# The end of a decoder layer: indirect gathers moved ahead and joined, the last two normalisation roots moved from GpSimd to ScalarE and VectorE, the last dense step split by tiles

## The chip, the core and the metric

The kernel runs on one core of a Trainium2 chip. The metric is the device time in microseconds of one execution, the median of several runs. Engines are called by the names of the profile: PE (TensorE), DVE (VectorE), ACT (ScalarE), POOL (GpSimd) and SP (SyncE, which issues plain DMAs here).

## What is computed

Input x has 8 sequences of 256 tokens with 128 features: 2048 tokens, which the kernel holds as 16 tiles of 128 tokens, in 4 groups of 4 tiles. Three layers follow one another, each with a residual and a layer norm: four blocks of elementwise linear attention with feed-forward, a cross attention with 16 heads, and a causal self attention with 16 heads and rotary positions, which is followed by a mixture of 31 experts of which each token takes its best 3, plus one shared expert. What the change touches is the end of that last layer:

```python
gates = jnp.sum(jax.nn.one_hot(topi, E_R, dtype=aff.dtype) * topv[..., None], axis=-2)
h = jax.nn.gelu(jnp.einsum('bsd,edh->besh', an, re_w1) + re_b1[None, :, None, :], approximate=False)
routed = jnp.einsum('bse,besh,ehd->bsd', gates, h, re_w2) + jnp.einsum('bse,ed->bsd', gates, re_b2)
return shared + routed + an + attn_out
# and outside: x = _layernorm(x + ffn(x)), (x - m) / sqrt(v + 1e-5) over the 128 features
```

## The kernel before

The program is written by hand: each engine has its own list of instructions, in order, and waits on semaphores that the others raise. All tiles have fixed places in on-chip memory; many share a large tensor "area", so the profile shows them under that name. `res`, the accumulator of the last layer, is "ntok" in the profile.

**Experts.** Groups 0 to 2 go through sorted slots. Each of the three chosen experts of a token has a slot, a row of the DRAM tensor `slot_in`; POOL scatters the token rows there with indirect DMAs during self attention (line 958). There are 68 slot tiles of 128 rows, worked off in 17 batches of 4 (`NBATCH`): SP loads a batch, PE turns it (L2324), DVE copies it (L1785), PE makes the hidden product (L2342), ACT the gelu (L1257), PE the output (L2358), DVE copies that (L1768) and SP stores it to the DRAM tensor `slot_out`. The semaphores `t_s[0..2]` count the landed stores of every third batch. The slot tiles of groups 0 and 1 (their 8 tiles of tokens, `SA`) are the first 55 of the 68 at most.

**Dense steps.** Group 3 is not sorted: it goes through the shared expert and all 31 experts, 32 steps numbered here 0 to 31 from `DENSE_K`. A step is a hidden product on PE (`hidden`, L2336, semaphore `m_h`), a gelu on ACT (L1253, `m_hg`), an output product on PE (`output`, L2355, `m_y`), and an add weighted by the gate on DVE (`add`, L1777, `m_a`, four instructions, one for each tile). PE runs one step ahead with the hidden product, and the banks of PSUM alternate. ACT's gelu k+2 and DVE's add k both wait for output k. The 35 gelus and 35 adds that the profile counts include three early steps.

**Gathers and combines.** When all slot outputs are stored, POOL gathers them back: for each group and each of the three choices four indirect DMAs (`gather`, L1031), one for each tile, 12 for a group, 36 in all. It does groups 0 and 1, then the root of group 0's norm, then the gathers of group 2, then the other roots. DVE adds what was gathered with the weight of the choice: nine combines (`combine`, L1795), placed behind given dense steps by the table `COMBINE_AFTER`: behind steps 8, 11, 14, 17, 20, 23, 26, 28 and 30. The gathered rows land where the loaded slot rows and their turned copies lie before, so that they may not land before the last slot hidden product has read these.

**Last norm.** For each group `last_stats` on DVE makes four `bn_stats` (L1841) and four `bn_aggr` (L1844) and raises `s_mv`; groups 0, 1, 2 behind dense steps 15, 24 and 30, group 3 behind the last. `last_root` on POOL makes minus mean, variance plus 1e-5, its power -0.5, and their product (L1039 to L1044). `last_apply` on ACT (L1321) then scales four tiles a group, in the order of the groups and behind all gelus; of group 3 ACT does two tiles and DVE the other two (L1865). SP stores each group (L711) and waits for the landing.

Of the kernel before, what the change touches and what calls it, by code (L numbers as in the profile page):

```python
# [4 lines left out]
B, S, D = 8, 256, 128  # L5
# [4 lines left out]
NG = B * S // GT  # L10
TPG = GT // 128
# [25 lines left out]
def program(nc, t, out):  # L37
# [7 lines left out]
    with ctx:  # L45
        def sb(name, shape, dt=f32):
            return ctx.enter_context(nc.sbuf_tensor(name, shape, dt))
# [128 lines left out]
        sq2 = sb("sq2", [128, TPG, D])  # L176
        ssm = sb("ssm", [128, 2, NT])
        sse = sb("sse", [128, 2, NT])
        rms = sb("rms", [128, 2, NT])
# [161 lines left out]
        s_vbb = sem("v_bias_loaded")  # L341
        s_ss = sem("square_sums_done")
        s_rms = sem("rms_steps_done")
# [35 lines left out]
        m_hg = sem("expert_gelu_done")  # L379
        m_y = sem("expert_output_done")  # L380
        m_a = sem("expert_output_added")
        s_out = sem("stored")
# [96 lines left out]
        def steps_of(g):  # L479
# [11 lines left out]
        COMBINE_AFTER = {DENSE_K + 8: 0, DENSE_K + 11: 1, DENSE_K + 14: 2, DENSE_K + 17: 3, DENSE_K + 20: 4, DENSE_K + 23: 5,  # L491
                         DENSE_K + 26: 6, DENSE_K + 28: 7, DENSE_K + 30: 8}
        STATS_AFTER = {DENSE_K + 15: 0, DENSE_K + 24: 1, DENSE_K + 30: 2}
        SCATTER_AT = {(2, 10): 2, (2, 11): 1, (2, 12): 2, (2, 13): 1, (2, 14): 2, (2, 15): 1, (2, 16): 2, (2, 17): 2,
                      (3, 0): 1, (3, 1): 1, (3, 2): 1, (3, 3): 1, (3, 4): 1, (3, 5): 1, (3, 6): 1, (3, 7): 1, (3, 8): 2, (3, 9): 1,
                      (3, 10): 2, (3, 11): 2, (3, 12): 2, (3, 13): 1, (3, 14): 1, (3, 15): 1, (3, 16): 3}
        NORMS = (0, 1, 2, 3)
        GATHERED = [(m_sc, 16 * 3 * ST)] + [(g_y[i], 0) for i in range(8)]

# [215 lines left out]
        def _(pool):  # L715
# [313 lines left out]
            def gather(g, j):  # L1029
                for i in range(g * TPG, (g + 1) * TPG):  # L1030
                    pool.indirect_dma_start(out=yg[:, j, i, :], out_offset=None, in_=slot_out,  # L1031
                                            in_offset=bass.IndirectOffsetOnAxis(ap=sloti[:, j, i:i + 1], axis=0))\
                        .then_inc(GATHERED[3 * g + j][0], 16)

            for r in range(3):
                pool.wait_ge(t_s[r], 16 * len(range(r, NBATCH, 3)))
            def last_root(i, g):
# [6 lines left out]
                pool.tensor_tensor(mneg[:, g, :], mneg[:, g, :], rstd[:, g, :], ALU.mult).then_inc(s_rs, 1)  # L1044

            for g in range(2):
                for j in range(3):
                    gather(g, j)
            last_root(0, 0)
            for j in range(3):  # L1050
                gather(2, j)
            for i, g in enumerate(NORMS[1:]):
                last_root(i + 1, g)

        @block.scalar
        def _(act):
# [260 lines left out]
            def last_apply(i, g, tiles):  # L1317
                act.wait_ge(s_rs, NG + 2 * i + 2)
                for q in tiles:
                    n = g * TPG + q  # L1320
                    last = act.activation(res[:, n, :], res[:, n, :], ACT.Identity, bias=mneg[:, g, q:q + 1],  # L1321
                                          scale=rstd[:, g, q:q + 1])
                last.then_inc(s_nt, 1)

            for i, g in enumerate(NORMS):
                last_apply(i, g, range(TPG) if i < 3 else range(2, TPG))

        @block.vector
        def _(dve):
# [509 lines left out]
            def last_stats(i, g):  # L1839
                for q in range(TPG):  # L1840
                    nc.vector.bn_stats(st[:, g, q, :], res[:, g * TPG + q, :]).then_inc(s_st, 1)  # L1841
                dve.wait_ge(s_st, TPG * (NG + i) + TPG)
                for q in range(TPG):
                    last = nc.vector.bn_aggr(mv[:, g, q, :], st[:, g, q, :])  # L1844
                last.then_inc(s_mv, 1)

            for k in range(1, len(STEPS)):
                if slot_batch(k + 2) is not None:
                    slot_inputs(slot_batch(k + 2))
                add(k)  # L1850
                if OWN.get(k) in ("logits", "b2"):
                    read_spare(NG - 1, (OWN[k], NG - 1), None)
                if OWN.get(k) in ("scale", "logits", "router", "choose"):
                    finish(OWN[k], NG - 1)
                if k in COMBINE_AFTER:
                    combine(COMBINE_AFTER[k])
                if k in STATS_AFTER:
                    dve.wait_ge(g_c, 3 * STATS_AFTER[k] + 3)
                    last_stats(STATS_AFTER[k], STATS_AFTER[k])
            dve.wait_ge(m_a, len(STEPS))  # L1860
            last_stats(3, 3)
            dve.wait_ge(s_rs, NG + 2 * 3 + 1)
            for q in range(2):
# [6 lines left out]
        def _(pe):  # L1870
# [475 lines left out]
            def output(k):  # L2346
# [5 lines left out]
                for i in range(TPG):  # L2352
                    h = hE[:, p, i * 128:(i + 1) * 128]
                    if kind == "dense":
                        last = nc.tensor.matmul(bank[2 + p][:, i * D:(i + 1) * D], h, we2[:, :] if e == E else experts[:, e, 1, :],  # L2355
                                                start=True, stop=True)
                    else:
# [106 lines left out]
```

## Time and profile before

| | us |
|---|---|
| median of 3 runs | 904.88 |
| lowest, highest | 903.38, 906.44 |
| the profiled execution | 905.01 |
| its span, first to last instruction | 903.2 |
| busy PE / DVE / ACT / POOL | 803.7 / 689.0 / 572.8 / 561.5 |
| mean granted clock of PE, share of full speed | 0.967 |

How to read it: the busy shares are averages over stages of different kinds. The change touches only the last 104 us, from the last slot batches at about 799 us on, so the profile is to be read there: the timeline of the single engines, and what ended their idle time. In the timeline a row can stand for several instructions in a row from one line (x4 is four). An idle time put down to "remote" or "another core or an unknown queue" is one whose releaser the profile did not find.

### The profile page before, as it was taken

The numbers are of one execution on the slowest core, as the hardware profiler recorded it, in microseconds if no ns is written. First come the engines' busy times: TensorE is split into PE (matmuls) and PEld (weight loads), VectorE is DVE, ScalarE is ACT, GpSimd is POOL, SyncE is SP. The second block draws the span as 40 slices with busy tenths as digits, with TensorE's granted clock in tenths as the row PEclk, the third lists the DMA queues.
The fourth block names the chain that finished last, engine by engine and source line by source line (L and its number), as shares of the span: only waits on it lengthen the run. The fifth ranks groups of instructions, "written<-read, shape, count | busy, mean of one in ns | idle before, by whom it ended". The sixth has DMA issues, their size and how long they took to land.

```text
span 903.2 us, 17391 instructions
## 1 busy us (share of the span) xinstructions
PE 803.7 (89%) x5325; PEld 531.4 (59%) x5325; DVE 689.0 (76%) x2494; ACT 572.8 (63%) x1445; POOL 561.5 (62%) x638
## 2 busy tenths in 40 slices
PE   5899999998789999999899999999988889893864
PEld 2344444444567677775466766766665568881643
DVE  4788888888879888899788599689949835651756
ACT  3678877884689999997566475476535653540324
POOL 5888888887641333333777496577969786437151
PEclk9899999999999999999999999999999999997888
DMA  8300000000051111001222122212222444532011
GB/s 235 109 1 0 1 1 0 1 1 0 1 135 54 54 53 43 2 2 48 53 69 68 48 55 65 68 40 59 76 59 59 132 150 132 174 108 53 4 36 47
DMA packets 57851, 51.88 MB, mean 57 GB/s; under 512 B 11586, under 2 KB 43042, under 8 KB 57762
## 3 DMA queue, kind: packets, MB, share of 16 engines
q1 hardware_dynamic: 55394, 46.05, 18.4%
q0 software_dynamic: 2304, 4.72, 1.8%
q8 instruction: 44, 0.72, 0.3%
q14 instruction: 45, 0.37, 0.1%
q10 hardware_dynamic: 64, 0.02, 0.0%
HBM read 21.66 MB, written 12.32 MB: 38 GB/s over the span
## 4 chain that ended last, share of the span: by engine, by line
PE 50%; POOL 19%; DVE 13%; issue 8%; ACT 5%; another core or an unknown queue 4%; ACTq 0%; DVEq 0%; POOLq 0%
PE psum L2028 5%; PE psum L2199 4%; DVE area L1482 4%; PE psum L2061 4%; POOL area L970 4%; PE psum L2045 3%; PE psum L2336 3%; PE psum L2355 3%; PE psum L2394 3%; PE psum L2087 3%; POOL area L879 3%; PE psum L2258 3%; PE psum L2372 2%; POOL slot_in L958 2%
## 5 line engine op out<-in xcount | busy, mean ns | idle before, releaser
L970 POOL TENSOR_TENSOR area<-area,rinv 128x512 f32<-128x512 f32 x64 | 94.2, 1472 | 69.2 <-DVE rinv L1803 68.8
L1275 ACT ACTIVATE area<-area,negmax 128x128 f32<-128x128 f32 (+1 forms) x256 | 112.8, 444 | 17.9 <-DVE negmax L1482 17.0
L1122 ACT ACTIVATE area<-area,negmax 128x256 f32<-128x256 f32 x256 | 108.8, 505 | 0.3
L1482 DVE CUSTOM_DVE_ANT_0 area<-psum,area 128x256 f32<-128x256 f32 x256 | 93.2, 420 | 17.6 <-PE psum L2013 16.8
L1470 DVE SCALAR_TENSOR_TENSOR area<-psum,ccol,cs 128x512 f32<-128x512 f32 x128 | 89.4, 740 | 21.1 <-PE psum L2061 20.9
L1482 DVE CUSTOM_DVE_ANT_0 area<-psum,maskc 128x128 f32<-128x128 f32 (+1 forms) x256 | 75.8, 351 | 9.8 <-issue 5.5
L2028 PE MATMUL psum<-ident,area 128*128 128x128 f32 x512 | 70.9, 279 | 9.1 <-DVE area L1522 7.6
L2061 PE MATMUL psum<-area,qkw 128*128 128x512 f32 x128 | 71.7, 642 | 7.7 <-DVE area L1470 5.0
L1777 DVE SCALAR_TENSOR_TENSOR ntok<-psum,gate,ntok 128x128 f32<-128x128 f32 x140 | 39.4, 343 | 44.8 <-remote 30.5
L2028 PEld LDWEIGHTS psum<-ident,area 128*128 128x128 f32 x512 | 56.9, 142 | 18.5 <-issue 11.1
L1265 ACT ACTIVATE area<-psum 128x512 f32<-128x512 f32 x32 | 19.1, 597 | 75.6 <-PE psum L2394 67.5
L1253 ACT ACTIVATE area<-psum,b1T 128x512 f32<-128x512 f32 x35 | 23.9, 686 | 67.2 <-PE psum L2336 35.6
L2372 PEld LDWEIGHTS psum<-ident,area 128*128 128x128 f32 x384 | 44.5, 141 | 35.1 <-issue 24.9
L2199 PE MATMUL psum<-area 128*128 128x512 f32 x128 | 63.6, 600 | 1.0
L2355 PEld LDWEIGHTS psum<-area 128*128 128x128 f32 x248 | 36.0, 212 | 43.6 <-ACT area L1253 30.4
L2087 PE MATMUL psum<-area 64*128 64x256 f32 (+1 forms) x512 | 60.1, 354 | 0.2 <-DVE negmax L1482 0.2
L2355 PE MATMUL psum<-area 128*128 128x128 f32 x248 | 37.3, 299 | 25.5 <-ACT area L1253 25.5
L770 POOL TENSOR_TENSOR ve<-mv,eps_o 128x2 f32<-128x2 f32 x8 | 1.7, 211 | 92.8 <-DVE mv L1444 92.8
L2372 PE MATMUL psum<-ident,area 128*128 128x128 f32 x384 | 53.5, 275 | 5.7 <-POOL area L970 4.6
L2190 PE MATMUL psum<-area 128*128 128x512 f32 x128 | 58.2, 594 | 0.3 <-ACT area L1177 0.3
L2394 PE MATMUL psum<-area 128*64 128x128 f32 x768 | 56.7, 283 | 0.0
L1582 DVE RECIPROCAL psum<-psum 128x512 f32<-128x512 f32 x16 | 53.7, 3355 | 0.0
(308 smaller groups left out, 2120.5 us busy)
## 6 DMA issues: line engine op xcount, KB each, us to landing
area<-area SPq DMA_DIRECT2D x256, 64.0 KB
slot_out<-area SPq DMA_DIRECT2D x17, 256.0 KB, 2.3
area<-slot_in SPq DMA_DIRECT2D x8, 512.0 KB, 4.1
slot_in<-gate SPq DMA_DIRECT2D x5, 768.0 KB, 4.6
area<-in_L_ffn_re_w SPq DMA_DIRECT2D x14, 256.0 KB
area<-in_mask_BxSxS_ik SPq DMA_DIRECT2D x8, 256.0 KB, 3.6
area<-in_L_attn_W SPq DMA_DIRECT2D x5, 256.0 KB, 6.1
area<-in_x SPq DMA_DIRECT2D x4, 256.0 KB, 3.5
```

What stands on the lines that cost most here:

```text
L970: pool.tensor_tensor(p4, p4, rinv[:, u % 4, 0:4].unsqueeze(2).to_broadcast([128, 4, w]), ALU.mult)\
L1122: last = act.activation(P[:, n % 4, r, mm, :], P[:, n % 4, r, mm, :], ACT.Exp, bias=negmax[:, n % 4, r, mm:mm + 1], scale=-1.0)
L1275: last = act.activation(Pc[:, u % 4, r, mm, 0:w], Pc[:, u % 4, r, mm, 0:w], ACT.Exp, bias=negmax[:, u % 4, r, mm:mm + 1], scale=-1.0, accu ...
L1470: last = nc.vector.scalar_tensor_tensor(rp[:, w, j, :].rearrange("p (b n) -> p b n", b=2), src.rearrange("p (b n) -> p b n", b=2), ccol[:, ...
L1482: return nc.vector.tensor_tensor_reduce(out=dst, in0=scores, in1=mask, scale=1.0, scalar=HIGHEST, op0=ALU.add, op1=ALU.min, accum_out=low)
L2028: last = nc.tensor.transpose(bank[4 + r][:, c:c + 128], P[:, n % 4, r, mm, kt * 128:(kt + 1) * 128], ident[:, :])
L2061: last = nc.tensor.matmul(dst, wt, xg, start=True, stop=True)
L2087: last = nc.tensor.matmul(heads[r][:, mm, :], QR[rows, hq % 2, mm, q * 128:(q + 1) * 128], KR[rows, hq % 2, mm, k0:k0 + w], start=True, st ...
L2199: last = nc.tensor.matmul(bank[6], w2[:, blk, j, :], hT[:, n % 2, j, :], start=(j == 0), stop=(j == FC - 1), skip_group_check=True)
L2355: last = nc.tensor.matmul(bank[2 + p][:, i * D:(i + 1) * D], h, we2[:, :] if e == E else experts[:, e, 1, :], start=True, stop=True)
L2372: last = nc.tensor.transpose(bank[4 + r][:, c:c + 128], Pc[:, u % 4, r, mm, kt * 128:(kt + 1) * 128], ident[:, :])
L2394: last = nc.tensor.matmul(bank[6][64 * r:64 * r + 64, c2:c2 + 128], Vc[:, hq % 2, 2 * (q // 2) + kt, (2 * mm + r) * HD:(2 * mm + r + 1) * HD],
```

## The change

Three things are changed.

1. **Gathers.** `EARLY_BATCHES` is 14, from (3 x 8 + 31) / 4 rounded up. POOL waits for the first 14 stored batches and for the last slot hidden product (`m_h`), issues the 24 gathers of groups 0 and 1, reading from the first 14 batches only, then waits for all stores and issues the 12 gathers of group 2, and only then the roots of groups 0 and 1.
2. **Roots of groups 2 and 3.** They leave POOL. ACT takes the square root of the variance plus 1e-5 (`last_deviation`), DVE its reciprocal and minus mean times that (`last_rstd`). A first square root without a reader is put ahead of the tiles of the last norm on ACT.
3. **Last dense step.** PE writes its four tiles to four banks and signals after each; DVE's adds (`last_add`) and statistics (`last_tile_stats`) of the single tiles alternate, with the reciprocal and mean of group 2 behind the first add. Combine 8 goes from behind step 30 to behind step 29.

```diff
-                         DENSE_K + 26: 6, DENSE_K + 28: 7, DENSE_K + 30: 8}
+                         DENSE_K + 26: 6, DENSE_K + 28: 7, DENSE_K + 29: 8}
+        EARLY_BATCHES = -(-(3 * SA + E) // 4)
+        LAST_BANK = (bank[2 + (len(STEPS) - 1) % 2], bank[4], bank[5], bank[6])
+        LAST_ORDER = (("add", 0), ("rstd", 2), ("negmean", 2), ("add", 1), ("add", 2), ("add", 3), ("rstd", 3), ("negmean", 3))
+        LAST_DONE = {what: i + 1 for i, what in enumerate(LAST_ORDER)}
...
@@ gpsimd
-                    pool.indirect_dma_start(out=yg[:, j, i, :], out_offset=None, in_=slot_out,
+                    pool.indirect_dma_start(out=yg[:, j, i, :], out_offset=None, in_=slot_out[0:EARLY_BATCHES * TPG * 128, :] if g < 2 else slot_out,
-            for r in range(3):
-                pool.wait_ge(t_s[r], 16 * len(range(r, NBATCH, 3)))
...
+            for r in range(3):
+                pool.wait_ge(t_s[r], 16 * len(range(r, EARLY_BATCHES, 3)))
+            pool.wait_ge(m_h, SLOT_K + NBATCH)
             for g in range(2):
                 for j in range(3):
                     gather(g, j)
-            last_root(0, 0)
+            for r in range(3):
+                pool.wait_ge(t_s[r], 16 * len(range(r, NBATCH, 3)))
             for j in range(3):
                 gather(2, j)
-            for i, g in enumerate(NORMS[1:]):
-                last_root(i + 1, g)
+            for i in range(2):
+                last_root(i, NORMS[i])
@@ scalar
             def last_apply(i, g, tiles):
-                act.wait_ge(s_rs, NG + 2 * i + 2)
+                if i < 2:
+                    act.wait_ge(s_rs, NG + 2 * i + 2)
+                else:
+                    act.wait_ge(l_a, LAST_DONE["negmean", i])
...
+            def last_deviation(i, g):
+                act.wait_ge(s_mv, NG + i + 1)
+                act.activation(sdev[:, i - 2, :], mv[:, g, :, 1], ACT.Sqrt, bias=eps_o[:, 0:1]).then_inc(s_ss, 1)
+
+            act.activation(sdev[:, 2, :], eps_o[:, 0:TPG], ACT.Sqrt)
             for i, g in enumerate(NORMS):
+                if i >= 2:
+                    last_deviation(i, g)
                 last_apply(i, g, range(TPG) if i < 3 else range(2, TPG))
@@ vector
+            def last_rstd(i, g):
+                dve.wait_ge(s_ss, NG + i - 1)
+                nc.vector.reciprocal(rstd[:, g, :], sdev[:, i - 2, :]).then_inc(l_a, 1)
+                dve.wait_ge(l_a, LAST_DONE["rstd", i])
+                nc.vector.scalar_tensor_tensor(mneg[:, g, :], mv[:, g, :, 0], -1.0, rstd[:, g, :], ALU.mult, ALU.mult)\
+                    .then_inc(l_a, 1)
+
+            def last_add(q):
+                k = len(STEPS) - 1
+                n = (NG - 1) * TPG + q
+                dve.wait_ge(m_a, k)
+                dve.wait_ge(m_y, k + q + 1)
+                nc.vector.scalar_tensor_tensor(res[:, n, :], LAST_BANK[q][:, 0:D], gate[:, n, STEPS[k][1]:STEPS[k][1] + 1],
+                                               res[:, n, :], ALU.mult, ALU.add).then_inc(l_a, 1)
+
+            def last_tile_stats(q):
+                dve.wait_ge(l_a, LAST_DONE["add", q])
+                nc.vector.bn_stats(st[:, NG - 1, q, :], res[:, (NG - 1) * TPG + q, :]).then_inc(s_st, 1)
+
-            for k in range(1, len(STEPS)):
+            for k in range(1, len(STEPS) - 1):
...
-            dve.wait_ge(m_a, len(STEPS))
-            last_stats(3, 3)
-            dve.wait_ge(s_rs, NG + 2 * 3 + 1)
+            last_add(0)
+            last_rstd(2, 2)
+            last_add(1)
+            last_tile_stats(0)
+            last_add(2)
+            last_tile_stats(1)
+            last_add(3)
+            last_tile_stats(2)
+            last_tile_stats(3)
+            last_moments(3, 3)
+            last_rstd(3, 3)
@@ tensor, output(k)
+                        dst = LAST_BANK[i][:, 0:D] if k == len(STEPS) - 1 else bank[2 + p][:, i * D:(i + 1) * D]
+                        last = nc.tensor.matmul(dst, h, we2[:, :] if e == E else experts[:, e, 1, :], start=True, stop=True)
+                        if k == len(STEPS) - 1 and i < TPG - 1:
+                            last.then_inc(m_y, 1)
```

## Rows read from the trace of the kernel before

**Rows 1.** Waits, 808 to 903.5 us: who waited for whom, us in total, times, longest.

```profile
ACT area L1253 <- remote: 30.5, 4, 16.1
DVE ntok L1777 <- remote: 30.5, 5, 12.9
```

**Rows 2.** Stretches: us long, busy us of each engine, PE clock, DMA share, GB/s.

```profile
812.50:839.30 26.80, 8.66 (x34) 5.25 (x33) 3.37 (x12) 2.06 (x3) 17.18 (x19) 0.69 0.18 47
...
864.00:874.30 10.30, 3.52 (x18) 1.86 (x17) 2.26 (x9) 0.86 (x2) 6.06 (x7) 0.97 0.19 47
```

**Rows 3.** Timeline of POOL: start, duration, what, idle before. First and last gathers, 24 and 12.

```profile
805.36 1.08 POOL L1031 DMA_INDIRECT area<-slot_out,area  x1 [10.26 <-DMA slot_out<-area]
...
834.22 0.94 POOL L1031 DMA_INDIRECT area<-slot_out,area  x1 [0.30 <-issue]
...
857.13 1.03 POOL L1031 DMA_INDIRECT area<-slot_out,area  x1 [0.16 <-issue]
...
870.94 0.94 POOL L1031 DMA_INDIRECT area<-slot_out,area  x1 [0.30 <-issue]
```

**Rows 4.** Timeline of PE and ACT: an output, a hidden product, the latter's gelu.

```profile
814.62 1.16 PE L2355 MATMUL psum<-area 128*128 128x128 f32 x8
815.61 1.02 PE L2336 MATMUL psum<-area 128*128 128x512 f32 x2
...
837.79 0.69 ACT L1253 ACTIVATE area<-psum,b1T 128x512 f32<-128x512 f32 x1 [16.15 <-remote]
```

**Rows 5.** Timeline of DVE: adds of dense steps 3, 4, 7, 11, 20, 23, 26.

```profile
808.59 1.12 DVE L1777 SCALAR_TENSOR_TENSOR ntok<-psum,gate,ntok 128x128 f32<-128x128 f32 x4 [0.63 <-PE psum L2355]
810.34 1.12 DVE L1777 SCALAR_TENSOR_TENSOR ntok<-psum,gate,ntok 128x128 f32<-128x128 f32 x4 [0.63 <-PE psum L2355]
...
832.95 1.12 DVE L1777 SCALAR_TENSOR_TENSOR ntok<-psum,gate,ntok 128x128 f32<-128x128 f32 x4 [12.91 <-remote]
...
845.48 1.12 DVE L1777 SCALAR_TENSOR_TENSOR ntok<-psum,gate,ntok 128x128 f32<-128x128 f32 x4 [0.50 <-PE psum L2355]
...
861.25 1.12 DVE L1777 SCALAR_TENSOR_TENSOR ntok<-psum,gate,ntok 128x128 f32<-128x128 f32 x4 [0.62 <-DVE ntok L1777]
...
874.29 1.13 DVE L1777 SCALAR_TENSOR_TENSOR ntok<-psum,gate,ntok 128x128 f32<-128x128 f32 x4 [1.77 <-remote]
...
882.40 1.13 DVE L1777 SCALAR_TENSOR_TENSOR ntok<-psum,gate,ntok 128x128 f32<-128x128 f32 x4 [0.81 <-PE psum L2355]
```

**Rows 6.** Timeline: copy of slot batch 13, last slot hidden product, copy of batch 16.

```profile
795.82 0.69 DVE L1768 COPY area<-psum 128x512 f32<-128x512 f32 x1 [0.94 <-PE psum L2358]
...
797.77 1.06 PE L2342 MATMUL psum<-area 128*128 128x128 f32 x8
...
801.58 0.69 DVE L1768 COPY area<-psum 128x512 f32<-128x512 f32 x1 [1.06 <-PE psum L2358]
```

**Rows 7.** Timeline of DVE, the end: add 30, combine 8, statistics of group 3.

```profile
889.41 1.13 DVE L1777 SCALAR_TENSOR_TENSOR ntok<-psum,gate,ntok 128x128 f32<-128x128 f32 x4 [0.30 <-PE psum L2355]
890.45 1.13 DVE L1795 SCALAR_TENSOR_TENSOR ntok<-area,ntok 128x128 f32<-128x128 f32 x4
...
893.95 0.87 DVE L1841 BATCH_NORM_STATS2 st<-ntok 128x6 f32<-128x128 f32 x4
894.85 0.38 DVE L1844 BATCH_NORM_AGGREGATE mv<-st 128x2 f32<-128x6 f32 x4
```

**Rows 8.** Timeline of ACT, the end: last gelu, tiles of groups 0 and 1, last two tiles.

```profile
888.45 0.69 ACT L1253 ACTIVATE area<-psum,b1T 128x512 f32<-128x512 f32 x1 [1.06 <-PE psum L2336]
889.03 3.17 ACT L1321 ACTIVATE ntok<-ntok,mneg,rstd 128x128 f32<-128x128 f32 x8
...
897.06 0.88 ACT L1321 ACTIVATE ntok<-ntok,mneg,rstd 128x128 f32<-128x128 f32 x2 [0.69 <-POOL mneg L1044]
```

**Rows 9.** Timeline of ACT: a table load, and the operation behind it.

```profile
768.29 1.28 ACT L1238 ACT_TABLE_LOAD   x1
769.58 0.31 ACT L1238 ACTIVATE area<-area 128x124 f32<-128x124 f32 x1
```

More of the change, by code:

```diff
@@ L177, in program @@
         ssm = sb("ssm", [128, 2, NT])
+        sdev = ssm[:, 0, 0:3 * TPG].rearrange("p (g t) -> p g t", t=TPG)
         sse = sb("sse", [128, 2, NT])
@@ L341, in program @@
         s_vbb = sem("v_bias_loaded")
-        s_ss = sem("square_sums_done")
+        s_ss = sem("square_sums_then_last_deviations_done")
         s_rms = sem("rms_steps_done")
@@ L380, in program @@
         m_y = sem("expert_output_done")
+        l_a = sem("last_vector_step_done")
         m_a = sem("expert_output_added")
@@ L1841, in last_stats, with last_moments @@
                     nc.vector.bn_stats(st[:, g, q, :], res[:, g * TPG + q, :]).then_inc(s_st, 1)
+                last_moments(i, g)
+            def last_moments(i, g):
                 dve.wait_ge(s_st, TPG * (NG + i) + TPG)
@@ L2354, in output @@
                     if kind == "dense":
-                        last = nc.tensor.matmul(bank[2 + p][:, i * D:(i + 1) * D], h, we2[:, :] if e == E else experts[:, e, 1, :],
-                                                start=True, stop=True)
+                        dst = LAST_BANK[i][:, 0:D] if k == len(STEPS) - 1 else bank[2 + p][:, i * D:(i + 1) * D]
+                        last = nc.tensor.matmul(dst, h, we2[:, :] if e == E else experts[:, e, 1, :], start=True, stop=True)
+                        if k == len(STEPS) - 1 and i < TPG - 1:
+                            last.then_inc(m_y, 1)
                     else:
```

## The prediction, made before the changed kernel was run

> **What bounds the kernel now.** I read the end of the run backwards, since the change touches only what happens after the slot batches. First the waits of the last 95 us: ScalarE's gelu (L1253) and VectorE's add (L1777) each lost 30.5 us to a releaser that the profile can't name, in four and five waits of up to 16.1 us [rows 1]. Those are the largest waits of the stage, so I looked at what happens in them. TensorE is nearly idle there: 8.66 us busy in 812.5 to 839.3, 3.52 us in 864.0 to 874.3, its clock partly at the lower level [rows 2]. On POOL both stretches lie inside a row of gathers: 24 in a row from 805.36 to 835.16 and 12 from 857.13 to 871.88, one every 1.25 us [rows 3]. Nothing in that stretch waits for gathered data: the first combine comes at add 8 of the dense steps.
>
> Who is late? TensorE finished the output of one step at 815.78 (814.62 + 1.16) and the next hidden product at 816.63 [rows 4], but the add that waits for that output began at 832.95 [rows 5] and the gelu that waits for that hidden product at 837.79 [rows 4]. ScalarE and VectorE had nothing else to wait for, and TensorE in its turn waited for that gelu. So signals of finished TensorE work come late while POOL issues gathers in a row. They are not late at once: adds still come every 1.75 us up to 810.34, five microseconds into the first row, and in the second row up to 861.25. Each row therefore has a free beginning, then almost no progress, then a restart at the lower clock.
>
> What each row costs, from the starts of the adds [rows 5], a normal step being 1.75 us (808.59 to 810.34):
> - 24 gathers: 810.34 to 845.48 is 7 steps. 35.14 - 7 x 1.75 = 22.9 us lost in a row of 29.8 us.
> - 12 gathers: 861.25 to 882.40 is 6 steps. 21.15 - 6 x 1.75 = 10.65 us lost in a row of 14.75 us.
> Together 33.55 us. The dense steps have no slack against this; every other microsecond up to the last add is the TensorE pace.
>
> **Part 1, earlier and joined gathers.** The old first gather waits for all 17 stores: the copy of batch 16 ends at 802.27 (801.58 + 0.69) and the gather starts 3.09 us later. The new one waits for store 13, whose copy ends at 796.51, so 799.60, and for the last slot batch's hidden product, which ends at 798.83 [rows 6]. Hence 799.6, 5.8 us earlier. That by itself is worth nothing: no combine waits for a gather. The last three stores are long landed when POOL asks for them, 30 us later, so that wait costs 0. What is queued behind it (12 gathers, two roots) is not late either: the first root's statistics come only after add 15.
>
> What changes is the shape: the root of group 0, for which POOL waited between the rows (835.16 to 857.13), goes behind the gathers. One row of 36 lasts 29.8 + 12 x 1.25 = 44.8 us, 799.6 to 844.4. No row of the trace has that length, so I bound it:
> - Straight line through the two rows: slope (22.9 - 10.65) / (29.8 - 14.75) = 0.814 per us, intercept -1.4. Lost: 0.814 x 44.8 - 1.4 = 35.1, **+1.5 us** against 33.55. I take this, as both lengths are measured.
> - By gathers (22.9 / 24 x 36 = 34.4): +0.8.
> - Upper: inside the first row VectorE stood idle for 12.91 us ahead of the add at 832.95 [rows 5]. If the added 15.0 us hold no progress at all: 22.9 + 15.0 = 37.9, **+4.4**.
> - Lower: between 861.25 and 874.29 three steps were made in 13.04 us, 40% of the pace. If the added time goes like that: 22.9 + 0.6 x 15.0 = 31.9, **-1.7**.
> The saved restart and the lost free beginning are both inside the line.
>
> **Part 2, the end.** In the run before: the last gelu ends at 889.14; VectorE idles 0.30 us ahead of add 30, then does combine 8, statistics of group 2, add 31, statistics of group 3, ending 895.23 [rows 7]; POOL's root takes until ScalarE can start its two last tiles at 897.06, and these end at 897.94 [rows 8]. Then store and landing, unchanged.
>
> VectorE after: combine 8 fills the idle, starting at 889.1 behind add 29. Add 30 at 890.15, statistics of group 2 from 891.2 (0.87 + 0.03 + 0.38) to 892.5, add of tile 0 until about 892.8. Then it needs ScalarE's square root of group 2.
>
> ScalarE after: a table load must precede the first square root. The gelu's end plus 1.28 [rows 9] is 890.4; the dummy root, 128x4, has no row: between 0.10 (one of four aggregations on VectorE, 0.38 / 4 [rows 7]) and 0.31 (ScalarE's 128x124 [rows 9]); I take 0.22, 890.65. Then the eight tiles of groups 0 and 1, 3.17 us [rows 8]: 893.8. Only then, in order, the root of group 2: 894.0. The statistics were ready at 892.5, but the root is queued behind that work, and VectorE stands in line for it, with three adds and all the statistics of group 3 behind: it loses about 1.2 us.
>
> From 894.05: reciprocal and mean 0.45 (two operations of 128x4 with waits; each lies between 0.10, an aggregation, and 0.28, an add, and I take 0.17), three adds at 0.26 and four statistics at 0.22 (four take 1.04 to 1.13 and 0.87 [rows 7]), aggregation 0.43: 896.6. Root on ScalarE and signal 0.3, reciprocal and mean 0.5, two tiles 0.88: 898.3. Against 897.94: **+0.4 us**. Had ScalarE been free, VectorE would go on at 892.8 and the same chain ends at about 897.05, **-0.9**: that is the worth of removing POOL's two roots. Tile-wise output brings nothing on top, since output 31 is ready at about 890.3 (gelu's end plus the 1.16 of an output [rows 4]) and VectorE comes at 892.5. The three added signals of TensorE and the other banks cost 0: nothing is queued behind them.
>
> Here the Trainium skill, ScalarE: Activation LUTs, section What ACT_TABLE_LOAD costs, speaks against the change: a switch of set is the load of about 1283 ns plus a drain of about 1380 ns. By that the end would be +1.8 rather than +0.4, a rival below. The trace agrees on the load and not on the drain: the operation behind the load at 768.29 starts at 769.58, 0.01 us after it [rows 9].
>
> **Sum.** Profiled execution 905.01 (span 903.2, 1.8 around it); + 1.5 + 0.4 = 906.9. The median of the runs is 904.88, 0.13 lower, which changes nothing. A measurement of this kernel can tell about 0.3%, 2.7 us, from no change.
>
> **Rivals.**
> - Forecast: the line, and the root queued behind the eight tiles: 906.9, its own range 904.5 to 909. Chance 0.43.
> - Slower: a long row holds TensorE's signals entirely. It decides from the point, some 15 us into a row, after which the first row shows almost 13 us without an add. 905.0 + 4.4 + 0.4 = 909.8. For: that gap. Against: a step did come through after it, before the last gather. Chance 0.20.
> - Faster: the stall is bound to a row's beginning and restart more than to its length, so that the 12 added gathers cost half of what they do now: 905.0 - 10.65 / 2 + 0.4 = 900.1. For: the second row pays a restart at the lower clock that a joined row pays once. Against: the losses of the two rows are almost in proportion (0.95 and 0.89 us for a gather). Chance 0.18.
> - The end does what it says: ScalarE's tiles of groups 0 and 1 are early enough, or the root overtakes nothing that matters: 905.0 + 1.5 - 0.9 = 905.6. Against: 3.17 us of tiles after a load of 1.28. Chance 0.16.
> - The switch of table costs twice its row, since ScalarE's pipeline has to be emptied as well; ScalarE is what VectorE waits for, so all of it counts: 905.0 + 1.5 + 0.4 + 1.3 = 908.2. Against: the gap of 0.01 us [rows 9]. Chance 0.03. This is the rule of the skill named above.
>
> The likeliest is 906.9. Faster by over 0.3%: the faster rival with a little of the lower bound, 0.22. Slower: the slower rival and the upper part of the forecast, 0.32. Within: 0.46. Range 899.5 to 910.5: it takes in both bounds of the long row and of the end, and leaves out what lies beyond the two outer rivals.
>
> **What would show it.** Gathers starting 3.1 us after the copy of batch 13; 36 of them at 1.25 us; adds at pace for six or seven microseconds, then few until three or four after the last gather, about 847; lost time 35 us in one stretch. In the end a table load behind the last gelu, the reciprocal of group 2 waiting for ScalarE 1 to 1.5 us, and the last tile ending 9.2 us after the last gelu (8.8 before). Wrong if TensorE goes on during the long row, or if the late signals come from something else than gathers in a row, which the trace shows only side by side.

## The result, and the profile after

The changed kernel takes 908.09 us (median of 12 executions), the kernel before 904.33 us beside it (12 executions): ratio 1.0042, 95% interval 1.0027 to 1.0056, 3.8 us slower. Forecast: 906.9, range 899.5 to 910.5. The profiled execution of after is one of the longest of the twelve, 910.85 us with a span of 909.1; the one before stood at 905.01 and 903.2. So the traces have to account for 5.9 us, of which 2.3 us lie ahead of the change: the copy of slot batch 16 starts at 803.87, against 801.58 [rows 6].

The waits after, 795 to 909 us (who waited for whom: total us, times, longest):

```profile
DVE ntok L1795 <- remote: 37.3, 3, 19.2
...
ACT area L1261 <- issue: 24.2, 2, 23.1
...
ACT area L1261 <- remote: 15.5, 2, 9.1
...
DVE rstd L1870 <- ACT ssm L1338: 1.7, 2, 1.3
```

These answer to [rows 1], where both engines stood at 30.5 us in waits of up to 16.1 us. DVE now has three for five, ACT 39.7 us in four (24.2 + 15.5), up to 23.1 us; for its longest the profile says "issue": it found no releaser at all.

POOL's timeline after (start, duration, instruction, idle before): first and last of the 36 gathers.

```profile
801.97 1.08 POOL L1037 DMA_INDIRECT area<-slot_out,area  x1 [4.58 <-PE psum L2390]
...
845.80 0.94 POOL L1037 DMA_INDIRECT area<-slot_out,area  x1 [0.30 <-issue]
```

The copy of batch 13 ends at 798.80, so the row starts 3.17 us after it. As releaser the profile names the last slot hidden product, which ends at 801.13, 0.84 us before the row; the landing of batch 13 is recorded only 0.1 us ahead of that signal, so the two conditions came almost together. The row lasts 44.8 us, as worked out.

DVE's timeline after, adds of dense steps 1 to 8 (the row "x8" holds steps 5 and 6), which answer to [rows 5]:

```profile
807.38 1.13 DVE L1795 SCALAR_TENSOR_TENSOR ntok<-psum,gate,ntok 128x128 f32<-128x128 f32 x4 [0.60 <-issue]
811.98 1.13 DVE L1795 SCALAR_TENSOR_TENSOR ntok<-psum,gate,ntok 128x128 f32<-128x128 f32 x4 [3.48 <-PE psum L2404]
819.01 1.13 DVE L1795 SCALAR_TENSOR_TENSOR ntok<-psum,gate,ntok 128x128 f32<-128x128 f32 x4 [5.90 <-remote]
839.32 1.13 DVE L1795 SCALAR_TENSOR_TENSOR ntok<-psum,gate,ntok 128x128 f32<-128x128 f32 x4 [19.18 <-remote]
852.64 2.29 DVE L1795 SCALAR_TENSOR_TENSOR ntok<-psum,gate,ntok 128x128 f32<-128x128 f32 x8 [12.19 <-remote]
856.06 1.13 DVE L1795 SCALAR_TENSOR_TENSOR ntok<-psum,gate,ntok 128x128 f32<-128x128 f32 x4 [1.14 <-PE psum L2404]
859.31 1.13 DVE L1795 SCALAR_TENSOR_TENSOR ntok<-psum,gate,ntok 128x128 f32<-128x128 f32 x4 [2.12 <-PE psum L2404]
```

Steps 1 to 8 take 51.93 us where seven steps take 12.25: 39.7 us lost, against 33.55 in the two rows of before. That is +6.15.

The end after, timelines of ACT and DVE, which answer to [rows 7, 8]:

```profile
896.89 0.69 ACT L1261 ACTIVATE area<-psum,b1T 128x512 f32<-128x512 f32 x1 [1.06 <-PE psum L2384]
897.59 1.28 ACT L1340 ACT_TABLE_LOAD   x1
898.88 0.20 ACT L1340 ACTIVATE ssm<-eps_o 128x4 f32<-128x4 f32 x1
899.00 3.17 ACT L1332 ACTIVATE ntok<-ntok,mneg,rstd 128x128 f32<-128x128 f32 x8
...
900.75 0.32 DVE L1880 SCALAR_TENSOR_TENSOR ntok<-psum,gate,ntok 128x128 f32<-128x128 f32 x1
902.07 0.28 ACT L1338 ACTIVATE ssm<-mv,eps_o 128x4 f32<-128x4 f32 x1
902.39 0.18 DVE L1870 RECIPROCAL rstd<-ssm 128x4 f32<-128x4 f32 x1 [1.32 <-ACT ssm L1338]
902.60 0.16 DVE L1872 SCALAR_TENSOR_TENSOR mneg<-mv,rstd 128x4 f32<-128x4 f32 x1
...
905.51 0.88 ACT L1332 ACTIVATE ntok<-ntok,mneg,rstd 128x128 f32<-128x128 f32 x2 [0.44 <-DVE mneg L1872]
```

From the end of the last gelu (897.58) to the end of the last tile (906.39) are 8.81 us; before, 8.80. But the span closes 2.7 us after the last tile (909.1 - 906.39), where before it closed 5.3 us after it (903.2 - 897.94). The balance of the two traces: 2.3 ahead of the change + 6.15 in the row + 0.0 to the last tile - 2.6 behind it = 5.9 us. I had not forecast the last term.

### The profile page after: what moved, and what is told of

Same layout as the page of the kernel before. It is cut to its first block, busy times and chain, and to the rows that moved or that the text cites. A ratio compares the mean times of both kernels' runs of the same rounds, so it can differ in the third digit from the quotient of the medians.

```text
span 909.1 us, 17396 instructions
## 1 busy us (share of the span) xinstructions
PE 804.1 (88%) x5325; PEld 530.8 (58%) x5325; DVE 689.2 (76%) x2498; ACT 575.2 (63%) x1449; POOL 558.1 (61%) x630
## 4 chain that ended last, share of the span: by engine, by line
PE 50%; POOL 18%; DVE 12%; issue 8%; ACT 6%; another core or an unknown queue 4%; ACTq 0%; DVEq 0%; POOLq 0%
PE psum L2076 5%; PE psum L2247 4%; DVE area L1500 4%; PE psum L2109 4%; POOL area L976 4%; PE psum L2093 3%; PE psum L2404 3%; PE psum L2384 3%; PE psum L2135 3%; PE psum L2444 3%; POOL area L885 3%; PE psum L2306 2%; PE psum L2422 2%; POOL slot_in L964 2%
## 5 line engine op out<-in xcount | busy, mean ns | idle before, releaser
L2404 PEld LDWEIGHTS psum<-area 128*128 128x128 f32 x248 | 35.4, 209 | 50.6 <-ACT area L1261 35.1
```

The source lines that it names most:

```text
L2404: last = nc.tensor.matmul(dst, h, we2[:, :] if e == E else experts[:, e, 1, :], start=True, stop=True)
```

## The experiments

One thing first: the kernel before took 904 to 908 us in three sessions on the chips, that of the result among them, and 867 us in three others. "Hold" below is short for what makes the difference: signals of finished TensorE work that arrive late. The time of the kernel before is named each time, and every comparison of times is inside one session; the one trace of the kernel before is from the session of the result. A ratio with an interval is the one on record; it is not the quotient of the two medians and can differ from it by 0.1% (913.38 / 907.56 is 1.0064, on record 1.0073).

**Session 1 (before 907.56 us): the parts, and the cause.** The gather part alone, with all four roots still on POOL:

```diff
...
+            for r in range(3):
+                pool.wait_ge(t_s[r], 16 * len(range(r, EARLY_BATCHES, 3)))
+            pool.wait_ge(m_h, SLOT_K + NBATCH)
             for g in range(2):
                 for j in range(3):
                     gather(g, j)
-            last_root(0, 0)
+            for r in range(3):
+                pool.wait_ge(t_s[r], 16 * len(range(r, NBATCH, 3)))
             for j in range(3):
                 gather(2, j)
-            for i, g in enumerate(NORMS[1:]):
-                last_root(i + 1, g)
+            for i, g in enumerate(NORMS):
+                last_root(i, g)
```

> The kernel before with the gather part of the change alone: the first 24 gathers behind 14 stored batches and the last slot hidden product, the 12 of group 2 directly behind them, all four roots on GpSimd as before. If the joined row of 36 gathers is what costs (TensorE's signals held back while it lasts), all of the loss of the full change is here: 3 to 6 us slower than before, ratio 1.003 to 1.007, and one stretch of about 40 us with hardly any add. If the loss comes from the end (table load, roots on two engines), this one is within 1 us of before.

Measured 913.38 us (5 executions), ratio 1.0073 (1.0057 to 1.0089): 5.8 us slower. DVE's timeline of this kernel, adds of steps 1 to 4:

```profile
803.88 1.13 DVE L1780 SCALAR_TENSOR_TENSOR ntok<-psum,gate,ntok 128x128 f32<-128x128 f32 x4 [0.59 <-issue]
810.01 1.12 DVE L1780 SCALAR_TENSOR_TENSOR ntok<-psum,gate,ntok 128x128 f32<-128x128 f32 x4 [5.01 <-issue]
824.84 1.12 DVE L1780 SCALAR_TENSOR_TENSOR ntok<-psum,gate,ntok 128x128 f32<-128x128 f32 x4 [13.70 <-remote]
847.94 1.13 DVE L1780 SCALAR_TENSOR_TENSOR ntok<-psum,gate,ntok 128x128 f32<-128x128 f32 x4 [21.98 <-remote]
```

Step 8 starts at 857.10: 53.22 - 12.25 = 41.0 us lost, against 33.55 in the two rows of before. All of the loss of the full change is in the gather part.

The end alone, gathers as before (the roots of groups 2 and 3 leave POOL, ACT and DVE do them, the last step goes by tiles):

```diff
             last_root(0, 0)
             for j in range(3):
                 gather(2, j)
-            for i, g in enumerate(NORMS[1:]):
-                last_root(i + 1, g)
+            last_root(1, NORMS[1])
...
+            act.activation(sdev[:, 2, :], eps_o[:, 0:TPG], ACT.Sqrt)
             for i, g in enumerate(NORMS):
+                if i >= 2:
+                    last_deviation(i, g)
                 last_apply(i, g, range(TPG) if i < 3 else range(2, TPG))
```

> The full change with the gathers as they were before: 24 behind all 17 stores, root of group 0, then 12. If the gather row is what costs, this one is within 1 us of before: the last two tiles end 8.8 us after the last gelu, as before, because the table load and the eight tiles of groups 0 and 1 delay the root of group 2 by 1.3 us and so take back what the removed GpSimd roots give (0.9 us). If the end is what costs, it is 3 us or more slower.

Measured 905.33 us (12), ratio 0.9974 (0.9960 to 0.9989): 2.2 us faster. Its two rows, of 24 and 12 gathers like those of before, lose 25.1 and 9.0 us, 34.1 in all (before: 22.9 and 10.65, 33.55 in all), so one row's loss differs by 2 us from trace to trace. Gelu to last tile is 8.82 us. So neither the row nor the chain to the last tile holds the gain; the stretch behind the last tile does, 2.7 us here (904.1 - 901.40) for 5.3. The two parts add up: +5.8 - 2.2 = +3.6, the whole change +3.8.

No gathers at all, and no wait of the combines for them (the combines add what lies there):

```diff
-            for g in range(2):
-                for j in range(3):
-                    gather(g, j)
-            last_root(0, 0)
-            for j in range(3):
-                gather(2, j)
-            for i, g in enumerate(NORMS[1:]):
-                last_root(i + 1, g)
+            for i, g in enumerate(NORMS):
+                last_root(i, g)
...
-                dve.wait_ge(GATHERED[q][0], GATHERED[q][1] + 16 * TPG)
```

> The kernel before without its 36 gathers; the combines read what lies in the place of the gathered rows, so the expert outputs of groups 0 to 2 are wrong. If the gathers are what holds TensorE's signals back, every add of the dense steps comes 1.75 us after the one before and the time falls by the 33.5 us that the two rows cost, to about 871. If the late signals have another cause in this stage (instruction loading, a power limit, the dense weights), long waits stay and the time falls by less than 10 us.

Measured 869.83 us (2), ratio 0.9589 (0.9567 to 0.9612): 37.7 us less. A stretch of its trace (us long, busy us of PE, PEld, DVE, ACT and POOL with the number of instructions, PE clock, DMA share, GB/s):

```profile
806.00:845.00 39.00, 39.00 (x227) 28.48 (x226) 31.06 (x119) 15.58 (x23) 1.58 (x4) 1.00 0.00 1
```

PE is busy throughout at the full granted clock, and the adds come every 1.75 us (806.92, 808.67, 810.42). The late signals of the dense steps are the gathers' doing: the prediction had seen them only side by side. Of the 37.7 us, 2.6 lie behind the last tile (table below), which leaves 35 for the rows.

24 gathers, one for each dense step; group 2's twelve and the waits for them left out:

```diff
+                    pool.wait_ge(m_a, DENSE_K + 1 + (3 * g + j) * TPG + i % TPG)
                     pool.indirect_dma_start(out=yg[:, j, i, :], out_offset=None, in_=slot_out,
```

> The kernel before with the 24 gathers of groups 0 and 1 spaced, one behind each dense step (GpSimd waits for one more add before each), and without the 12 of group 2, so that part of group 2 is wrong. If it takes gathers back to back to hold TensorE's signals, no add is late by more than 1 us and the time is near that of no_gathers, about 871 to 875. If each gather has its price however it is spaced, the 24 cost 22.9 us as they do in a row, and the time is about 894.

Measured 873.70 us (one execution). The same stretch, and the one add-up that came late (DVE's timeline):

```profile
806.00:845.00 39.00, 38.74 (x222) 27.90 (x221) 30.75 (x117) 15.09 (x23) 21.45 (x23) 1.00 0.15 38
```

```profile
848.09 1.14 DVE L1794 SCALAR_TENSOR_TENSOR ntok<-area,ntok 128x128 f32<-128x128 f32 x4 [2.85 <-DMA area<-slot_out,area]
```

No wait for an unnamed releaser is left in the dense steps. The last tile ends 3.05 us later than without gathers (867.64 against 864.59), where two combines wait for their rows (2.85 and 1.07 us), since at one gather a step the data come too late; another 1.6 us lie behind the last tile (table below). It is not the gathers as such that hold TensorE but how they follow each other. This is one execution, but against 907 us the gap is no matter of spread, and the execution itself was one with hold, as its scatters show (below).

**Session 2 (before 867.49 us): how dense may a row be?** Four kernels, all with the early gathers of the first experiment and different spacing; of the diffs only the lines that space are shown. Six gathers in five steps:

```diff
+                    n = (3 * g + j) * TPG + i % TPG
+                    pool.wait_ge(m_a, DENSE_K - 2 + 5 * n // 6)
                     pool.indirect_dma_start(out=yg[:, j, i, :], out_offset=None,
```

> All 36 gathers, early start as in the change, but spaced: GpSimd waits before each for the add of a dense step, six gathers in five steps, 1.46 us on average where the row has 1.25. Roots as before. If it takes gathers strictly back to back to hold TensorE's signals, this slight spacing is enough: no add late by more than a microsecond, time 870 to 876. If it is the rate of gathers over some microseconds, and 1.75 us (free in paced_24) is slow enough but 1.46 is not, part of the 33 us stays and the time is 880 to 900.

Four in three steps, and bursts of four:

```diff
+                    pool.wait_ge(m_a, DENSE_K - 2 + 3 * n // 4)
...
+                    pool.wait_ge(m_a, DENSE_K - 2 + 10 * (n // 4) // 3)
```

> As paced_6in5, but four gathers in three steps, 1.31 us on average, a duty of GpSimd of 95%. If a single gap now and then clears the way for TensorE's signals, 870 to 880. If the rate counts, most of the loss of the row of 36 stays: 890 to 910. Since a held signal also holds the adds that pace the gathers, the row should stretch itself once it is held, so I expect the middle, 875 to 895.

> As paced_6in5 in rate, but the wait stands only before every fourth gather: bursts of four back to back, then a pause of about 0.8 us. If held signals need six or more gathers in a row to build up (as both rows of the kernel before show) and a short pause resets that, time 870 to 876. If the pause is too short to reset it, 880 or more.

And a small memset on POOL ahead of each gather, without spacing them:

```diff
+                    pool.memset(sq2[:, 0, 3 * n:3 * n + 3], 0.0)
```

> The joined row of 36, no wait in it, but a small memset on GpSimd before each gather, which spaces them to about 1.45 to 1.6 us. If spacing alone lets TensorE's signals through, the time is that of paced_6in5. If it is the wait for an add (a row that yields to the dense steps) that helps, and not the spacing, the loss is that of the row of 36, 905 to 912.

Measured: 867.99 us (10 executions), ratio 0.9996 (0.9983 to 1.0009); 866.93; 867.52; 867.34 (one each). They tell nothing apart, because in session 2 nothing was held: the kernel before itself took 867.49. Nor are the three spaced kernels spaced everywhere: six in five starts with five gathers in a row (798.20 to 803.34), and the first twelve of the bursts come at 1.24 to 1.39 us (795.83 to 809.80). The most telling is the memset, which fits into the 0.30 us gap and leaves a dense row of 36. POOL's timeline of that kernel, second and third gather:

```profile
796.98 0.96 POOL L1034 DMA_INDIRECT area<-slot_out,area  x1 [0.18 <-issue]
798.24 0.95 POOL L1034 DMA_INDIRECT area<-slot_out,area  x1 [0.19 <-issue]
```

One every 1.26 us, and not one late add. I had taken the hold for a property of the kernel; it is one of the kernel and the session.

**Session 3 (another chip, before 867.78 us).** The spaced row again, and the dense row of the first experiment again, word for word the same kernel:

> The same kernel as paced_6in5, beside the kernel before on the same chip. On the chip of the last runs no row of gathers held anything (kernel before 867.5, and a row of 36 at 1.26 us without one late add), so that the spacing could not be judged. If this chip is like that, both kernels take about 867 and the ratio is 0.998 to 1.001. If it is like the chip where the kernel before took 907.6: with gathers spaced to 1.46 us on average enough to let TensorE's signals through, 870 to 878 (ratio about 0.965); if the rate counts and 1.46 is too fast, 885 to 905.

> The same kernel as gathers_only, the joined row of 36 gathers with the end as before. On a chip whose rows hold TensorE's signals: 4 to 7 us slower than before. On a chip where they don't: 867 like the kernel before, since no combine waits for a gather and 5.8 us earlier is worth nothing.

Measured 867.81 us (10), ratio 0.9996 (0.9985 to 1.0007), and 867.98 us (8), ratio 0.9998 (0.9986 to 1.0011). The kernel that took 913.38 us in session 1 takes 867.98 here. Its stretch, the first and last of its gathers, and two adds inside the row:

```profile
806.00:845.00 39.00, 39.00 (x226) 28.48 (x225) 32.37 (x128) 15.48 (x23) 28.65 (x35) 1.00 0.19 50
```

```profile
796.40 1.08 POOL L1032 DMA_INDIRECT area<-slot_out,area  x1 [4.58 <-PE psum L2345]
...
840.37 0.94 POOL L1032 DMA_INDIRECT area<-slot_out,area  x1 [0.30 <-issue]
```

```profile
810.58 1.13 DVE L1780 SCALAR_TENSOR_TENSOR ntok<-psum,gate,ntok 128x128 f32<-128x128 f32 x4 [0.62 <-PE psum L2358]
812.33 1.13 DVE L1780 SCALAR_TENSOR_TENSOR ntok<-psum,gate,ntok 128x128 f32<-128x128 f32 x4 [0.62 <-PE psum L2358]
```

The row is as dense and as long (36 in 44.9 us) and moves as many bytes (50 GB/s in this stretch, 52 in session 1), and TensorE works through it at 1.75 us a step. Here the joined row is worth nothing either way: its early start buys nothing, as the prediction had it.

**Sessions 4 and 5 (one chip, some minutes apart).** The spaced row a third time, then the full change again:

> The same kernel as paced_6in5, once more beside the kernel before, to meet a chip whose rows of gathers hold TensorE's signals. On such a chip (kernel before at 903 to 908): 870 to 878 if spacing to 1.46 us on average is enough, 885 to 905 if the rate counts. On a chip without it: 867 for both.

> The full change beside the kernel before on another chip. On a chip where rows of gathers hold nothing (kernel before at 867), the gather part is worth 0, so that this ratio is that of the end alone: within 0.1% of 1, since the two-engine roots and the wait behind ScalarE's eight tiles cancel (8.8 us from last gelu to last tile in both). If the 0.26% that end_only gained on the other chip were a gain of the end itself, the ratio here is 0.997. On a chip whose rows hold TensorE's signals (kernel before at 903 to 908): 1.004 as measured before.

Session 4: before 867.44 us, the spaced row 868.87 (10 executions; one of them took 2646.97 us, which nothing here explains), ratio 1.0010 (0.9997 to 1.0024). Session 5, same chip: before 906.52 us (17 executions), the changed kernel 910.05 (12), ratio 1.0035 (1.0019 to 1.0050). So the chip is not what makes the difference. In session 5 the full change loses 41.0 us in the row (adds of steps 1 and 8 at 804.86 and 858.13), takes 8.81 us from gelu to last tile and 2.7 us from there to the end of the span: the first result once more. Its longest single wait:

```profile
847.47 1.13 DVE L1795 SCALAR_TENSOR_TENSOR ntok<-psum,gate,ntok 128x128 f32<-128x128 f32 x4 [24.78 <-remote]
```

**The hold reaches the scatters too.** In self attention, 140 us ahead of the dense steps, POOL issues five indirect scatters in a row, one every 1.26 us. ACT's wait at that place, in the trace of before and in that of the dense row of session 3:

```profile
667.64 0.60 ACT L1265 ACTIVATE area<-psum 128x512 f32<-128x512 f32 x1 [8.01 <-remote]
```

```profile
665.04 0.60 ACT L1268 ACTIVATE area<-psum 128x512 f32<-128x512 f32 x1 [4.73 <-PE psum L2397]
```

All seven traces of sessions with hold have this wait of 8.0 to 8.4 us for an unnamed releaser, none of the seven others has it. From the first scatter to the copy of slot batch 16 the former take 166.3 to 166.7 us (before: 635.22 to 801.58), the latter 162.3 to 162.4. So these 4 us go with the hold as well, the kernels without gathers and with 24 were run under it, and each trace tells by itself which kind of session it comes from.

**The stretch behind the last tile**, from the spans and the timelines of ACT and POOL of eight kernels:

| kernel | gathers | POOL's last operation ends, before the last tile does | from last tile to the end of the span |
|---|---|---|---|
| before | 36 | 0.9 us | 5.3 us |
| gather part alone | 36 | 0.9 us | 5.3 us |
| the same, session 3 | 36 | 0.9 us | 5.3 us |
| 24 gathers, spaced | 24 | 0.9 us | 4.3 us |
| no gathers | 0 | 0.9 us | 2.7 us |
| end alone | 36 | 15.6 us | 2.7 us |
| after | 36 | 14.6 us | 2.7 us |
| after, session 5 | 36 | 14.6 us | 2.7 us |

The six other traces with 36 gathers and all roots on POOL, spaced or with the memset, close in 5.2 to 5.3 us. How such a line is read: the first line of the page and the last rows of POOL's and ACT's timelines, of the kernel without gathers, then of that with 24. Last tile at 864.59 and 867.64, end of the span at 867.3 and 871.9.

```profile
span 867.3 us, 17347 instructions
```

```profile
863.47 0.20 POOL L1044 TENSOR_TENSOR mneg<-mneg,rstd 128x4 f32<-128x4 f32 x1
863.71 0.88 ACT L1315 ACTIVATE ntok<-ntok,mneg,rstd 128x128 f32<-128x128 f32 x2 [0.68 <-POOL mneg L1044]
```

```profile
span 871.9 us, 17377 instructions
```

```profile
866.52 0.20 POOL L1045 TENSOR_TENSOR mneg<-mneg,rstd 128x4 f32<-128x4 f32 x1
866.76 0.88 ACT L1319 ACTIVATE ntok<-ntok,mneg,rstd 128x128 f32<-128x128 f32 x2 [0.68 <-POOL mneg L1045]
```

The span ends about 0.1 us after the last increment of one semaphore, in which the engines seem to report at the program's close. In the traces' semaphore records this increment comes 0.25 us after the last store has landed where POOL ended early or issued no gathers, 1.85 us after it with 24 gathers and 2.82 us with 36; the differences are those of the table. The kernels with no and with 24 gathers have POOL's roots as late as before, so it isn't the roots alone. What fits all of it: POOL has work of its own left from the gathers, about 0.08 us for each (0.97 us for 12), that starts only when its last instruction is done. If POOL's instructions end some 15 us earlier, it lies beside other work. That the late report is POOL's is inferred from which kernels show it; the record names no engine. The Trainium skill, Runtime: NRT & Kernel Launch, section The ~15µs preamble/postamble breakdown, has a closing barrier that waits for all engines, at about 1.5 us; the traces agree that something is waited for there, show that it can come 2.6 us later (2.82 for 0.25), and do not show the 1.5 us as a length of their own.

## Why the prediction was right, and where it was not

- **What bounds the end: right, and now shown** for sessions with hold. Without gathers 37.7 us are gone and no signal of the dense steps is late.
- **Start of the row: right.** 3.17 us after the copy of batch 13 for 3.09, row of 44.8 us. The wait for the hidden product, which the prediction put 0.8 us ahead of the store, ends together with it, since 0.84 us pass from the product's end to the first gather. That the early start is worth nothing by itself: right where nothing is held (0.9998).
- **The joined row, +1.5 us: too small.** It measured +6.15 in the profile of after, and the gather part alone +5.8 us by medians. The failed step is the slope of the straight line through the two rows, 0.81 us lost per added us: 35.1 us lost predicted; 39.7, 41.0 and 41.0 measured. Two points of one trace did not carry it: the same two rows in the trace of the end alone (25.1 and 9.0 us) give a slope of 1.07 and 41.2 us. In fact the adds show two lengths with one behaviour: before, steps 5, 6 and 7 were added between 810.34 and the row's end; after, steps 2, 3 and 4 between 807.38 and 846.74. Three steps in either case, so the added 15 us held no progress at all (two steps each in the first row of the end alone, in the gather part alone and in session 5). That was the slower rival's mechanism, at 0.20. Its price of 37.9 was too low as well, by 1.8 us and more: behind the row the fourth add came 12.6 us after its end, against 10.3 us before (845.48 - 835.16). Of these 2.25 us, 1.75 lie ahead of the first add behind the row (852.64 is 5.90 us after the row's end, 839.31 was 4.15), and 0.50 in the three steps that follow. In the 21 us behind the row the granted clock was 0.71, against 0.81 behind the first row of before, so after the longer standstill TensorE worked more of the restart at the lower of its two levels (1.2 and 2.4 GHz); which part of the 2.25 us that is, the traces don't separate. The stretches of after (columns as above), the row and what follows it:

```profile
802.00:846.70 44.70, 15.81 (x75) 10.22 (x74) 7.01 (x22) 5.20 (x9) 34.03 (x36) 0.68 0.26 69
846.70:867.70 21.00, 17.16 (x78) 12.19 (x78) 10.94 (x40) 5.29 (x8) 0.04 (x1) 0.71 0.02 5
```

Under hold, two short rows (33.55, 34.1) were cheaper than one long one.
- **The end to the last tile, +0.4 us: right in kind, 0.4 too dear.** All of it is there: the load behind the last gelu, no pause behind the load (0.01 us, so no drain, as the row of before had said), the root of group 2 behind the eight tiles, DVE waiting 1.32 us for it where 1.2 was forecast. The chain from the reciprocal to the end of the last tile took 4.00 us (902.39 to 906.39); I had 4.25, among it reciprocal and mean at 0.37 for 0.45; the other 0.1 lies ahead of it.
- **"Then store and landing, unchanged": wrong by -2.6 us.** I ended my reading at the last tile. The span and the last tile of before were both on the page, and 5.3 us between them is 3 us more than the 2.3 us to landing that its DMA table gives for these stores; asking for the rest would have shown that the close waits for something other than the stores. The runs point to POOL, which the change takes away from the end. It is the one gain of the change. With it the rearranged end is worth 2.2 us (0.9974, 0.9960 to 0.9989), not +0.4.
- **The sum.** 1.5 + 0.4 = 1.9 stood for about 5.8 - 2.2 = 3.6 by medians. Two larger errors partly cancelled: the row cost over 4 us more, the close gave 2.6 us back. The forecast of 906.9 came 1.2 us from the median of 908.09 with that help, and with 0.7 us more from a start at 905.01, where the kernel before took 904.33 beside it; as a difference it was 1.9 for a measured 3.8. Landing so near was in part luck. Of the rivals, "slower" was nearest to the truth about the row. "The end does what it says" had the sign of the end right, but not by its mechanism: the root of group 2 did wait behind the eight tiles (1.32 us), and the gain came behind the last tile.

**What stays open.** What switches the hold on. It is not the kernel (the same one took 913.38 and 867.98), not the chip (867.44, then 906.52), not the gathers' rate, length or bytes, which are the same in both. Whatever it is stays the same for a whole session, for all kernels in it. Nor is it separated whether POOL's issuing or the transfers that it starts hold the signals: leaving out the gathers takes both away. Every execution on record comes with its span and granted clock, so was traced; whether the hold exists in one that is not, no run shows. Whether a row at 1.45 us a gather (50.8 us from the first start to the last) is enough to avoid the hold also stays open, the more so as it has runs of five and held scatters came five in a row: the three sessions in which it ran were ones without hold, where it cost nothing (0.9996, 0.9996, 1.0010). One gather in 1.75 us did avoid it. The best complete kernel of the sessions with hold is the end alone, 0.9974 of before. Joined to spaced gathers it wasn't tried.

## What to carry to other kernels

Do not extrapolate a stall along a line through two lengths of one trace: count how many steps get through it, since a longer one may let no more through. Space indirect gathers that run beside a TensorE chain by waiting on the chain's own progress; one to a step was enough here. Run the unchanged kernel in every session before tuning for a time that may depend on the session. And follow the accounting to the last microsecond of the span: an engine that has issued gathers should have its last instruction well before the end.

## What the runs showed of the hardware

- **A row of indirect gathers can hold TensorE's signals.** With one gather every 1.25 us, adds keep their pace for five microseconds and then wait up to 24.78 us for products that PE finished long before (the add at 847.47 in session 5 for an output of 812.39 to 814.47). At about 1.75 us a gather no signal of PE is late (one run). A row of five scatters at 1.26 us holds one for 8.0 us. In other sessions the dense rows hold nothing.
- **The records mark those sessions.** Four gathers raise a semaphore by 64 in all. In the seven traces without hold all 64 are there, but for one semaphore that shows 61. In sessions with hold the eight semaphores of before show 5 to 18 each, of after 3 to 15; the spaced 24 gathers, which held nothing up, still show 37 to 58. The combines that wait for the full 64 do start, so it is only records that are missing; but whoever sees "remote" as releaser can look there for a crowded path of signals. That the same path delays TensorE's signals is an inference.
- **POOL seems to have work left after gathers**, about 0.08 us for each, behind its last instruction: with it 0.9 us ahead of the last tile the span closes in 5.3 us with 36 gathers, 4.3 with 24 and 2.7 with none, and in 2.7 with 36 where POOL ends 15 us earlier.
- **A gather costs POOL 0.94 us and leaves a gap of 0.30 us**, into which a small memset fits at almost no cost (1.26 us a gather instead of 1.25).
